# Moving the split of a group's row maxima from VectorE to GpSimd in a fused attention and expert block

## The chip, the cores and the metric

The kernel runs on one core of one Trainium2 chip. The metric is the device time of one launch in microseconds (us), the median of several runs. TensorE (PE) has its weight loads shown apart (PEld). VectorE is DVE, ScalarE is ACT, GpSimd is POOL, and SyncE (SP) only issues DMAs here. SPq and ACTq are the DMA issues from those two queues. Each engine works through its own list of instructions in order. Engines meet only at semaphores.

## What is computed

Four batches of 512 tokens of width 256 pass through a gated cross-attention and then a gated block of self-attention and experts. Both attentions have 16 heads of width 16:

```python
x = x + tanh(g_xattn) * xattn(layernorm(x), ctx, ctx, wq, bq, wk, bk, wv, bv)
x = x + tanh(g_ffn) * ffn(layernorm(x), ...)
# both attentions:
scores = einsum("bhld,bhsd->bhls", q, k) / 4
attn = softmax(scores, axis=-1)
out = einsum("bhls,bhsd->bhld", attn, v)
# ffn after its attention: rmsnorm(src + sa), shared swiglu experts,
# 8 routed experts in 2 groups, the best 2 of the best group, rmsnorm
```

## The kernel before

There are eight attention instances (four cross, then four self), and each has four **groups** of four heads: 32 groups, numbered 0 to 31 here. A group is worked through in 16 **steps** (4 tiles of keys by 4 heads). At each step PE makes one tile of transposed scores (the unit, L1754) and ACT takes its exponential (L949). After four of these PE multiplies them with the values (L1717, eight rows in the trace).

The exponential needs the row maxima of the scores beforehand. So PE also makes every score tile the other way round, 12 pairs ahead (L1689, two matmuls for a pair), and DVE takes the maximum of each row out of PSUM (L1205, writing `negm`). A pair goes through a ring of two bank pairs in PSUM. PE may fill one only when DVE has released the pair before last. Pairs are filled at the odd steps. A group's eighth and last pair is filled at step 7 of the group before it.

When all maxima of a group are there, they are parted into two bf16 numbers. `m2` (the trace calls it `m`) gets the rounded maximum (L1213, CAST) and then the rest of it (L1214, TENSOR_TENSOR), both 128 partitions by 16 elements. PE turns `m2` with one transpose (L1696, the **turn**) at step 9 (`AT_MAX`), ACT copies the result (L837), and at step 11 (`AT_ROWS`) ACT's queue issues two small DMAs (L846) that put the rows into the stack of queries. The first unit of the next group waits for these.

In between, at step 8 (`AT_HEADS`), PE turns the finished heads of the group before (L1703) through the same ring, and DVE divides them by their sums (L1226, L1227) and releases the bank. The next ring pair on PE waits for that.

What DVE has at a group's end, in its list: the maximum of the eighth pair (step 7), the two parts, the heads (step 8), the maximum of the next pair (step 9).

POOL does the parts of the projections (L684, L689, L694, 128 by 1024 elements each), the scale of each row of a norm (`row_scale`, a chain of small operations that ends in L677 or L679), the sum of heads (L704, L705) and, early on, a long row of memsets and iotas for the sorting at the end (`constants`). A table of hooks sets at which step of which group each piece is written on each engine. `link` on POOL and DVE lets an operation finish before the next one starts.

SP's list is in order too. While instance 0 runs it loads the stacks of groups 2 and 3, each when the rows of an earlier group have landed (`s_mrow`, L548 to L556). Only then does it store instance 1's parts to DRAM (L532, L538) and load them back as stacks.

Of the kernel before, what the change touches and what calls it, by code (L numbers as in the profile page):

```python
# [10 lines left out]
ALU = mybir.AluOpType  # L11
# [7 lines left out]
MPART = 2  # L19
# [3 lines left out]
LEAD = 12  # L23
FILL, FILL_STACK, FILL_ROWS = 24, 12, 10
PROB_SLOTS = 3
AT_COPY, AT_HEADS, AT_MAX, AT_ROWS = 4, 8, 9, 11
SCORE_BANKS = [0, 1, 7]
END_BANKS = [0, 1, 7, 6, 2, 3, 4, 5]

# [7 lines left out]
def flamingo_block(nc, x, ctx_in, g_xattn, g_ffn, wq, bq, wk, bk, wv, bv,  # L37
# [7 lines left out]
    NG = NH // HG  # L45
# [4 lines left out]
    EPG = NE // NGRP  # L50
# [13 lines left out]
    PAIRS = NH * TT // 2  # L64
    UNITS = NH * TT
    STEPS = UNITS // NG
# [5 lines left out]
    MROWS = MPART * HG * TT  # L72
# [5 lines left out]
    GROUPS = NI * NG  # L78
    N_PAIRS = NI * PAIRS
# [30 lines left out]
    for n in range(1, NI):  # L110
        m = n + 1
# [22 lines left out]
    for u_ in range(NI * UNITS):  # L134
        n_, g_, s_ = u_ // UNITS, u_ // STEPS % NG, u_ % STEPS
# [99 lines left out]
    with es:  # L235
        def sb(name, shape, dt):
            return es.enter_context(nc.sbuf_tensor(name, shape, dt))

        def sem(name):
            return es.enter_context(nc.semaphore(name))  # L240
# [58 lines left out]
        negm = sb("negm", [P, 2, HG, TT], F32)  # L299

        m2 = sb("m2", [P, 2, P], BF16)
# [91 lines left out]
        s_re = sem("ring_emptied")  # L393
        s_m2 = sem("maximum_parts")
# [32 lines left out]
        s_ini = sem("dve_setup_chain")  # L427
# [2 lines left out]
        block = es.enter_context(nc.Block())  # L430


        turned, taken = [], LEAD
        for gi_ in range(GROUPS):
            for s_ in range(STEPS):
                taken += s_ % 2 and (gi_ * STEPS + s_) // 2 + LEAD < N_PAIRS
                if s_ == AT_HEADS and gi_ > 0:
                    taken += 1
                    turned.append(taken)
# [31 lines left out]
        def group_inst(gi):  # L471
            return INST[gi // NG]
# [171 lines left out]
        def _(pool):  # L644
            k = [0]

            def link(ins):
                k[0] += 1
                ins.then_inc(s_pool, 1)
                pool.wait_ge(s_pool, k[0])  # L650
# [41 lines left out]
            def third_part(m, X):  # L692
                pool.wait_ge(s_p1[X], m + 1)
                link(pool.tensor_tensor(parts[X][:, 2], qk[X][:], parts[X][:, 1], ALU.subtract))  # L694
                pool.sem_inc(s_spl[X], 1)
# [3 lines left out]
            def add_heads(b, g):  # L699
# [6 lines left out]
                if g == NG - 1:  # L706
                    pool.sem_inc(s_x1, 1)

            def stats(m):
                kind, b = INST[m]  # L710
                row_scale(b, "x" if kind == "c" else "x1")
# [41 lines left out]
            for X in (1, 0):  # L753
                rest(1, X)
                third_part(1, X)
            pool.wait_ge(s_tg, 1)
            pool.memset(fg[:, :, NR:RW], 0.0).then_inc(s_cst, 1)
            constants()
            for n in range(NI):
                for g in range(NG):  # L760
                    gi = n * NG + g
                    for s in range(STEPS):
                        if s == AT_HEADS and gi > 0 and group_inst(gi - 1)[0] == "c":
                            add_heads(group_inst(gi - 1)[1], (gi - 1) % NG)
                        for what, m, i in HOOKS.get((n, g, s), []):
                            if what == "stats":
                                stats(m)
                            elif what == "sum":
                                rotated_sum(m, i)
                            elif what == "rest":  # L770
                                rest(m, i)
                            elif what == "part2":
                                third_part(m, i)
                            elif what == "fastats":
                                row_scale(m, "y")
# [253 lines left out]
        def _(dve):  # L1029
            k = [0]  # L1030

            def mark(ins):
                k[0] += 1
                ins.then_inc(s_dve, 1)

            def settle():
                dve.wait_ge(s_dve, k[0])

            def link(ins):
                mark(ins)  # L1040
                settle()

            def ready(s):
                settle()
                dve.sem_inc(s, 1)  # L1045

            V = nc.vector
# [152 lines left out]
            def row_max(q):  # L1200
                gi, p = divmod(q, PAIRS // NG)
                h, tt = divmod(p, TT)
                c, bank = ring.take()
                dve.wait_ge(s_rf, c + 1)
                V.tensor_reduce(negm[:, gi % 2, h::2, tt], ps[:, bank:bank + 2, :], AX.X, ALU.max,  # L1205
                                negate=True).then_inc(s_re, 1)
                if p + 1 == PAIRS // NG:
                    dve.wait_ge(s_re, c + 1)
                    if gi == 0:
                        dve.wait_ge(s_ini, 5 + EPG)  # L1210
                    m = negm[:, gi % 2].rearrange("p (a h) t -> p a (h t)", a=2)
                    o = m2[:, gi % 2, 0:MROWS].rearrange("p (a s r) -> p s a r", a=2, s=MPART)
                    link(V.tensor_copy(o[:, 0], m))  # L1213
                    mark(V.tensor_tensor(o[:, 1], m, o[:, 0], ALU.subtract))  # L1214
                    ready(s_m2)

            def heads_out(gi):
                kind, b = group_inst(gi)
# [35 lines left out]
            for n in range(NI):  # L1254
                for g in range(NG):
                    gi = n * NG + g
# [705 lines left out]
```

## Time and profile before

| | |
|---|---|
| median of 3 runs | 764.12 us (764.07 to 764.27) |
| the profiled execution, its own time | 764.05 us |
| its span, first to last instruction | 762.3 us |
| time outside the span | 1.75 us |
| PE busy, share of the span | 94% |
| DVE busy | 66% |
| ACT busy | 55% |
| POOL busy | 29% |
| mean granted clock of PE | 0.989 |

The attention with its 32 groups fills the span up to about 523 us; the experts follow. A row of the timeline gives the start in us from the span's start, the duration in us, engine, line, operation, output and input, shapes, how many instructions are merged in it, and in brackets how long the engine was idle before it and what ended that. A matmul row's duration is modelled. Weight loads (PEld) are apart from one another by about 0.23 us even when nothing is waited for, so such a row says that PE waits only where it stands clearly above that. A row of a grouped view gives busy us and mean ns of one instruction behind the first bar, and idle us before it behind the second.

### The profile page before, as it was taken

To read this page: it belongs to the slowest core of one execution; us is meant where nothing else is said; L and a number is where in the kernel's file an instruction comes from. 1 tells how busy PE (TensorE), PEld (TensorE's weight loads), DVE (VectorE), ACT (ScalarE), POOL (GpSimd) and SP (SyncE) were. 2 spreads that over 40 slices of the span, in tenths; PEclk is the share of its full clock that TensorE was granted. 3 is DMA by queue.
4 is the path that set the end of the run, shared out by engine and by line. 5 is a ranking of instruction groups with operands and counts; after the bars stand their busy time and mean duration, and the time that the engine had idled before them with its cause. 6 is when DMAs were issued, how large, how long until landed. Compare 5 with 4: busy or idle time off the path is not lost.

```text
span 762.3 us, 10523 instructions
## 1 busy us (share of the span) xinstructions
PE 718.1 (94%) x3470; PEld 319.1 (42%) x3512; DVE 505.9 (66%) x743; ACT 416.2 (55%) x800; POOL 221.7 (29%) x328
## 2 busy tenths in 40 slices
PE   8798999999999999999989999999999999999995
PEld 5432233243232233233323332424544856468884
DVE  5598758956968978977797789771476122533554
ACT  4356868777767876875775867676211122222111
POOL 7343133314305415303321510010104722400444
PEclk9999999999999999999999999999999999999998
DMA  8516514216214413322331332006002655000001
GB/s 262 186 43 213 162 51 166 85 39 208 80 43 157 146 46 121 118 82 83 108 92 43 107 112 75 10 3 209 12 1 112 215 176 166 0 1 0 36 35 42
DMA packets 61172, 73.33 MB, mean 96 GB/s; under 512 B 10944, under 2 KB 46016, under 8 KB 61120
## 3 DMA queue, kind: packets, MB, share of 16 engines
q1 hardware_dynamic: 56464, 63.81, 27.1%
q0 software_dynamic: 2816, 8.46, 3.0%
q10 hardware_dynamic: 1840, 0.40, 0.3%
q8 instruction: 29, 0.48, 0.3%
q14 instruction: 23, 0.19, 0.1%
HBM read 45.04 MB, written 27.33 MB: 95 GB/s over the span
## 4 chain that ended last, share of the span: by engine, by line
PE 65%; DVE 13%; ACT 8%; DMA 4%; issue 4%; SPq 2%; POOL 2%; ACTq 0%; POOLq 0%; DVEq 0%
PE ps L1558 30%; PE ps L1717 12%; PE ps L1754 11%; DVE negm L1205 7%; PE ps L1689 6%; ACT hS L949 5%; PE ps L1553 3%; POOL scrf L779 2%; DMA scrq<-mix 1%; DVE bst L1083 1%; PE ps L1703 1%; PE ps L1617 1%; DMA rows<-in_L_xattn_wq_dram 1%; DMA w<-scrq 1%; PE ps L1648 1%
## 5 line engine op out<-in xcount | busy, mean ns | idle before, releaser
L1205 DVE TENSOR_REDUCE negm<-ps 128x2 f32<-128x1024 f32 x256 | 302.7, 1221 | 67.0 <-PE ps L1689 58.5
L949 ACT ACTIVATE hS<-ps 128x512 f32<-128x512 f32 x512 | 280.4, 605 | 105.4 <-PE ps L1754 98.3
L1754 PE MATMUL ps<-w 98*128 98x512 bf16 (+1 forms) x470 | 160.7, 387 | 15.6 <-ACT hS L949 9.8
L1717 PE MATMUL ps<-hS,mix 128*17 128x512 f32 x1024 | 136.4, 605 | 0.2
L1689 PE MATMUL ps<-w 64*128 64x512 bf16 x512 | 100.3, 389 | 9.7 <-DVE negm L1205 4.9
L1754 PEld LDWEIGHTS ps<-w 98*128 98x128 bf16 (+1 forms) x512 | 43.5, 96 | 156.8 <-ACT hS L949 86.1
L1406 DVE SCALAR_TENSOR_TENSOR ctxs<-qk,ps 128x512 f32<-128x512 f32 x32 | 22.0, 687 | 72.4 <-ACT qk L985 71.6
L1689 PEld LDWEIGHTS ps<-w 64*128 64x128 bf16 x512 | 24.7, 93 | 95.4 <-issue 68.9
L985 ACT ACTIVATE qk<-ps 128x512 f32<-128x512 f32 x32 | 19.1, 597 | 76.3 <-PE ps L1558 76.3
L1558 PE MATMUL ps<-w,hS 128*128 x256 | 55.6, 379 | 0.0
L1558 PEld LDWEIGHTS ps<-w,hS 128*128 128x128 f32 x256 | 48.6, 190 | 7.0 <-issue 0.5
L666 POOL TENSOR_TENSOR mdif<-bst 128x4 f32<-128x4 f32 x12 | 2.5, 205 | 142.4 <-DVEq L1045 142.4
L689 POOL TENSOR_TENSOR qk<-qk,mix 128x1024 f32<-128x1024 f32 x14 | 29.8, 2131 | 47.8 <-ACT mix L869 47.4
L704 POOL TENSOR_SCALAR hS<-hS,tg 128x256 f32<-128x256 f32 x16 | 14.8, 928 | 92.2 <-DVEq L1231 92.2
L684 POOL TENSOR_TENSOR qk<-qk,hT 128x1024 f32<-128x1024 f32 x8 | 18.8, 2349 | 75.3 <-DVEq L1045 75.3
L694 POOL TENSOR_TENSOR mix<-qk,mix 128x1024 bf16<-128x1024 f32 x14 | 29.8, 2131 | 21.1 <-ACT mix L873 20.0
L1025 ACT ACTIVATE tmp<-mix 128x257 f32<-128x257 f32 x16 | 6.7, 418 | 49.9 <-DVE mix L1438 49.9
L1717 PEld LDWEIGHTS ps<-hS,mix 128*17 128x17 f32 x1024 | 17.0, 95 | 30.1 <-ACT hS L949 14.8
L1409 DVE SCALAR_TENSOR_TENSOR hS<-ctxs,ps 128x512 f32<-128x512 f32 x32 | 22.0, 687 | 10.3 <-PE ps L1558 10.0
L1558 PE MATMUL ps<-cT,fin 128*128 128x512 f32 x64 | 28.4, 594 | 0.3 <-ACT cT L978 0.3
L1558 PE MATMUL ps<-rope_sb,fin 128*128 128x512 f32 x64 | 28.4, 594 | 0.0
L779 POOL DMA_INDIRECT scrf<-rows,place x16 | 16.2, 1014 | 41.3 <-DVEq L1045 36.8
(220 smaller groups left out, 893.5 us busy)
## 6 DMA issues: line engine op xcount, KB each, us to landing
w<-scrk SPq DMA_DIRECT2D x192, 64.0 KB, 2.0
w<-scrq SPq DMA_DIRECT2D x64, 128.0 KB, 2.5
scrk<-mix SPq DMA_DIRECT2D x24, 256.0 KB, 2.5
scrq<-mix SPq DMA_DIRECT2D x16, 384.0 KB, 3.5
scrq<-mix SPq DMA_DIRECT2D x24, 256.0 KB, 2.5
w<-scrq SPq DMA_DIRECT2D x64, 64.0 KB, 2.5
w<-in_L_ffn_W_experts_dram SPq DMA_DIRECT2D x8, 512.0 KB, 8.2
mix<-scrf SPq DMA_DIRECT2D x4, 528.0 KB, 3.8
```

What stands on the lines that cost most here:

```text
L689: link(pool.tensor_tensor(qk[X][:], qk[X][:], parts[X][:, 0], ALU.subtract))
L694: link(pool.tensor_tensor(parts[X][:, 2], qk[X][:], parts[X][:, 1], ALU.subtract))
L779: pool.indirect_dma_start(dst[:], bass.IndirectOffsetOnAxis(ap=place[:, tile:tile + 1], axis=0), source, None).then_inc(done, 16)
L949: nc.scalar.activation(prob[:, kt % PROB_SLOTS, s % HG, :], slot_bank(("unit", u)), ACT.Exp, scale=SC).then_inc(s_exp, 1)
L1205: V.tensor_reduce(negm[:, gi % 2, h::2, tt], ps[:, bank:bank + 2, :], AX.X, ALU.max, negate=True).then_inc(s_re, 1)
L1406: V.scalar_tensor_tensor(out=uu[:, k % 2, :], in0=th[k % 4], scalar=1.0, in1=end_full(f"{name}{b}", 2 * p), op0=ALU.add, op1=ALU.mult).the ...
L1409: V.scalar_tensor_tensor(out=hS[:, b * TT:(b + 1) * TT, p, :], in0=uu[:, k % 2, :].rearrange("p (t j) -> p t j", t=TT), scalar=0.5, in1=en ...
L1553: last = TR(o[:, tt * P:(tt + 1) * P], t[:, tt, c * P:(c + 1) * P], identf[:])
L1558: last = MM(o, w, r, start=(j == 0), stop=(j == len(terms) - 1))
L1689: last = MM(ps[:, bank + kind, :], qs[at:at + MAIN, g, hh, tt * P:(tt + 1) * P], ks[at:at + MAIN, g, hh, :], start=True, stop=True)
L1717: last = MM(ps[32 * h:32 * h + VM, 6, :], vp[n % 2][:, kt, g * HG + h, :], prob[:, kk % PROB_SLOTS, h, :], start=(kt == 0), stop=(kt == TT ...
L1754: MM(o, ks[0:rows, g, h, kt * P:(kt + 1) * P], qs[0:rows, g, h, :], start=True, stop=True).then_inc(s_sT, 1)
```

## The change

The two operations leave `row_max` on DVE and become `max_parts` on POOL, with the same operands. They wait there for the release of the last pair of the group (`RING_AT` gives its number in the ring). They stand ahead of step 7's hooks of the group before (`AT_PARTS`); those of group 0 stand between POOL's parts of the keys and of the queries in the beginning.

```diff
-AT_COPY, AT_HEADS, AT_MAX, AT_ROWS = 4, 8, 9, 11
+AT_COPY, AT_PARTS, AT_HEADS, AT_MAX, AT_ROWS = 4, 7, 8, 9, 11
...
+        RING_AT = list(range(LEAD))
         turned, taken = [], LEAD
         for gi_ in range(GROUPS):
             for s_ in range(STEPS):
-                taken += s_ % 2 and (gi_ * STEPS + s_) // 2 + LEAD < N_PAIRS
+                if s_ % 2 and (gi_ * STEPS + s_) // 2 + LEAD < N_PAIRS:
+                    RING_AT.append(taken)
+                    taken += 1
...
+            def max_parts(gi):
+
+                pool.wait_ge(s_re, RING_AT[(gi + 1) * PAIRS // NG - 1] + 1)
+                if gi == 0:
+                    pool.wait_ge(s_ini, 5 + EPG)
+                m = negm[:, gi % 2].rearrange("p (a h) t -> p a (h t)", a=2)
+                o = m2[:, gi % 2, 0:MROWS].rearrange("p (a s r) -> p s a r", a=2, s=MPART)
+                link(pool.tensor_copy(o[:, 0], m))
+                link(pool.tensor_tensor(o[:, 1], m, o[:, 0], ALU.subtract))
+                pool.sem_inc(s_m2, 1)
...
             for X in (1, 0):
                 rest(1, X)
                 third_part(1, X)
+                if X:
+                    max_parts(0)
             pool.wait_ge(s_tg, 1)
             pool.memset(fg[:, :, NR:RW], 0.0).then_inc(s_cst, 1)
             constants()
...
                     for s in range(STEPS):
+                        if s == AT_PARTS and gi + 1 < GROUPS:
+                            max_parts(gi + 1)
                         if s == AT_HEADS and gi > 0 and group_inst(gi - 1)[0] == "c":
                             add_heads(group_inst(gi - 1)[1], (gi - 1) % NG)
...
                 V.tensor_reduce(negm[:, gi % 2, h::2, tt], ps[:, bank:bank + 2, :], AX.X, ALU.max,
                                 negate=True).then_inc(s_re, 1)
-                if p + 1 == PAIRS // NG:
-                    dve.wait_ge(s_re, c + 1)
-                    if gi == 0:
-                        dve.wait_ge(s_ini, 5 + EPG)
-                    m = negm[:, gi % 2].rearrange("p (a h) t -> p a (h t)", a=2)
-                    o = m2[:, gi % 2, 0:MROWS].rearrange("p (a s r) -> p s a r", a=2, s=MPART)
-                    link(V.tensor_copy(o[:, 0], m))
-                    mark(V.tensor_tensor(o[:, 1], m, o[:, 0], ALU.subtract))
-                    ready(s_m2)
```

Below, three places in the order of instructions. The semaphores in brackets are by their names in the program: `ring_emptied` is DVE's release of a pair, `pool_chain` and `dve_chain` are the `link` of the two engines, `x1_row_statistics` tells POOL that DVE has the statistics of a norm. The line numbers of the changed kernel are higher by 3 on POOL up to L711, by 14 after `max_parts`, and by 18 or 9 on DVE.

POOL's list at the end of the constants, in the beginning, before:

```order
L742 MEMSET tabs 128x1
L743 MEMSET tabs 128x2
L744 MEMSET tabs 128x1
L704 TENSOR_SCALAR hS<-hS,tg 128x4x64 [waits heads_ready]
L705 TENSOR_TENSOR rows<-rows,hS 128x4x64 [waits pool_chain]
```

and of the changed kernel:

```order
L756 MEMSET tabs 128x1
L757 MEMSET tabs 128x2
L758 MEMSET tabs 128x1
L719 CAST m<-negm 128x2x8 [waits ring_emptied]
L720 TENSOR_TENSOR m<-negm,m 128x2x8 [waits pool_chain]
L719 CAST m<-negm 128x2x8 [waits pool_chain,ring_emptied]
L720 TENSOR_TENSOR m<-negm,m 128x2x8 [waits pool_chain]
L707 TENSOR_SCALAR hS<-hS,tg 128x4x64 [waits pool_chain,heads_ready]
```

The parts of groups 1 and 2 now stand behind the last memset of the constants.

POOL's list around the `row_scale` of a self-attention norm (group 19's turn follows it), before:

```order
L672 TENSOR_SCALAR mdif<-mdif 128x4 [waits pool_chain]
L673 TENSOR_TENSOR nvar<-nvar,mdif 128x4 [waits pool_chain]
L677 TENSOR_TENSOR scale<-nvar,mhalf 128x4 [waits pool_chain]
L679 TENSOR_TENSOR shift<-mean,scale 128x4 [waits pool_chain]
L684 TENSOR_TENSOR qk<-qk,hT 128x1024 [waits pool_chain,rotation_ready0]
```

and of the changed kernel:

```order
L676 TENSOR_TENSOR nvar<-nvar,mdif 128x4 [waits pool_chain]
L680 TENSOR_TENSOR scale<-nvar,mhalf 128x4 [waits pool_chain]
L682 TENSOR_TENSOR shift<-mean,scale 128x4 [waits pool_chain]
L719 CAST m<-negm 128x2x8 [waits pool_chain,ring_emptied]
L720 TENSOR_TENSOR m<-negm,m 128x2x8 [waits pool_chain]
L719 CAST m<-negm 128x2x8 [waits pool_chain,ring_emptied]
L720 TENSOR_TENSOR m<-negm,m 128x2x8 [waits pool_chain]
L687 TENSOR_TENSOR qk<-qk,hT 128x1024 [waits pool_chain,rotation_ready0]
```

The parts of group 19 come after the whole chain of the norm's scale.

DVE's list at the end of a group, before:

```order
L1205 TENSOR_REDUCE negm<-ps 128x2 [waits ring_full]
L1213 CAST m<-negm 128x2x8 [waits ring_emptied]
L1214 TENSOR_TENSOR m<-negm,m 128x2x8 [waits dve_chain]
L1226 RECIPROCAL rec<-ps 128x16 [waits dve_chain,ring_full]
L1227 TENSOR_TENSOR hS<-ps,rec 128x4x64 [waits dve_chain]
L1205 TENSOR_REDUCE negm<-ps 128x2 [waits ring_full,ring_emptied]
```

and of the changed kernel:

```order
L1223 TENSOR_REDUCE negm<-ps 128x2 [waits ring_full]
L1235 RECIPROCAL rec<-ps 128x16 [waits ring_full]
L1236 TENSOR_TENSOR hS<-ps,rec 128x4x64 [waits dve_chain]
L1223 TENSOR_REDUCE negm<-ps 128x2 [waits ring_full,ring_emptied]
```

The reciprocal of the heads follows the last maximum directly. PE's list is the same in both.

## Rows read from the trace of the kernel before

**Rows 1.** The page: engines' busy time and share; the chain that ended last, by engine

```profile
PE 718.1 (94%) x3470; PEld 319.1 (42%) x3512; DVE 505.9 (66%) x743; ACT 416.2 (55%) x800; POOL 221.7 (29%) x328
...
PE 65%; DVE 13%; ACT 8%; DMA 4%; issue 4%; SPq 2%; POOL 2%; ACTq 0%; POOLq 0%; DVEq 0%
```

**Rows 2.** Groups of instructions on DVE: the two parts

```profile
L1213 DVE CAST m<-negm 128x16 bf16<-128x16 f32 x32 | 11.7, 366 | 1.1
...
L1214 DVE TENSOR_TENSOR m<-negm,m 128x16 bf16<-128x16 f32 x32 | 5.6, 175 | 1.1
```

**Rows 3.** Timeline at the turn of group 19, behind a norm's `row_scale`

```profile
323.88 1.22 DVE L1205 TENSOR_REDUCE negm<-ps 128x2 f32<-128x1024 f32 x1
...
325.13 0.17 DVE L1213 CAST m<-negm 128x16 bf16<-128x16 f32 x1
...
325.34 0.17 DVE L1214 TENSOR_TENSOR m<-negm,m 128x16 bf16<-128x16 f32 x1
...
325.63 0.10 PEld L1696 LDWEIGHTS ps<-identb,m 128*128 128x128 bf16 x1 [0.29 <-DVEq L1045]
...
325.76 0.20 POOL L679 TENSOR_TENSOR shift<-mean,scale 128x4 f32<-128x4 f32 x1
...
326.43 0.10 PEld L1689 LDWEIGHTS ps<-w 64*128 64x128 bf16 x2 [0.63 <-DVE hS L1227]
```

**Rows 4.** Groups of instructions on POOL and on DVE: prices of elementwise work

```profile
L694 POOL TENSOR_TENSOR mix<-qk,mix 128x1024 bf16<-128x1024 f32 x14 | 29.8, 2131 | 21.1 <-ACT mix L873 20.0 <-POOL mix L694 0.7 <-POOL rows L705 0.4
...
L705 POOL TENSOR_TENSOR rows<-rows,hS 128x256 f32<-128x256 f32 x16 | 11.6, 726 | 1.3
...
L666 POOL TENSOR_TENSOR mdif<-bst 128x4 f32<-128x4 f32 x12 | 2.5, 205 | 142.4 <-DVEq L1045 142.4
```

```profile
L1110 DVE TENSOR_TENSOR mix<-qk,mix 128x1024 bf16<-128x1024 f32 x2 | 2.5, 1226 | 0.3
```

**Rows 5.** Timeline at the turn of group 1: DVE, PEld and the last constant

```profile
55.17 0.17 DVE L1213 CAST m<-negm 128x16 bf16<-128x16 f32 x1
...
56.63 0.10 PEld L1696 LDWEIGHTS ps<-identb,m 128*128 128x128 bf16 x1 [0.34 <-issue]
```

```profile
59.51 0.10 POOL L744 MEMSET tabs<- 128x1 f32 x1
```

**Rows 6.** Chain that ended last at 58 us, and PEld at the stack's load

```profile
58.10 1.78 DMA w<-mTs
```

```profile
83.34 0.10 PEld L1689 LDWEIGHTS ps<-w 64*128 64x128 bf16 x2 [0.50 <-DMA w<-scrq]
```

**Rows 7.** Timeline: pauses of DVE and PE in the beginning

```profile
44.41 1.23 DVE L1205 TENSOR_REDUCE negm<-ps 128x2 f32<-128x1024 f32 x1 [0.56 <-DVE m L1214]
```

```profile
50.67 0.39 PE L1689 MATMUL ps<-w 64*128 64x512 bf16 x2 [1.05 <-DVE negm L1205]
```

```profile
75.28 0.59 PE L1754 MATMUL ps<-w 98*128 98x512 bf16 x2 [2.05 <-DMA w<-mTs]
```

**Rows 8.** Busy time by stretch: busy us (count) of each engine, PEclk, DMA share, GB/s

```profile
77.00:80.00 3.00, 3.00 (x14) 0.37 (x12) 1.59 (x2) 1.28 (x4) 0.29 (x2) 0.50 0.78 266
```

**Rows 9.** Timeline at the turn of group 17, with POOL at work

```profile
298.50 2.13 POOL L689 TENSOR_TENSOR qk<-qk,mix 128x1024 f32<-128x1024 f32 x1 [1.22 <-ACT mix L869]
299.07 1.59 DVE L1213 CAST m<-negm 128x16 bf16<-128x16 f32 x1
...
301.03 0.10 PEld L1696 LDWEIGHTS ps<-identb,m 128*128 128x128 bf16 x1 [0.23 <-DVEq L1045]
```

```profile
301.77 0.39 PE L1754 MATMUL ps<-w 128*128 128x512 bf16 x1 [0.50 <-ACT hS L949]
```

**Rows 10.** Timeline at the turn of group 29, with nothing else in the way

```profile
479.07 0.10 PEld L1696 LDWEIGHTS ps<-identb,m 128*128 128x128 bf16 x1 [0.23 <-DVEq L1045]
...
479.51 0.39 PE L1754 MATMUL ps<-w 128*128 128x512 bf16 x1 [0.21 <-ACT hS L949]
```

**Rows 11.** Timeline behind the turn of group 27: PE waits for DVE's ring

```profile
461.15 0.39 PE L1689 MATMUL ps<-w 64*128 64x512 bf16 x2 [0.72 <-DVE negm L1205]
```

## The prediction

> **What bounds the kernel now.** I read the page first: PE is busy 94% of the span and holds 65% of the chain that ended last, DVE 66% and 13% [rows 1]. PE runs its list in order, so what matters is whether a step of PE starts later or earlier, not how busy DVE is. DVE's share of the chain is the second thing to see: there are stretches in which PE waits for the ring. Then I read the groups of DVE for what leaves it: 32 casts of 0.366 us in the mean and 32 subtractions of 0.175 us, 17.3 us in all [rows 2]. Last I went through the timeline at all 32 turns, because the two operations have one consumer, the turn on PE. The question at each is what ends last there: the parts, PE's own work before the turn, or something else.
>
> Three kinds of turn are to be seen. In the plain kind [rows 10] the turn comes 0.23 us after the weight load before it, PE's usual spacing, so the parts are just in time or early, and 0.4 us later PE stands still for 0.21 us for an exponential that does not depend on the turn. In the second kind the parts are late: at group 19 the last maximum ends at 325.10, the parts at 325.51, and PE's load follows at 325.63, 0.53 us behind the maximum [rows 3]. In the third kind POOL is in the way: at group 17 a cast of normally 0.175 us takes 1.59 us and ends with POOL's operation, at 300.66 against 300.63 [rows 9].
>
> **What leaves DVE.** Two operations and their joints. At group 19 the cast starts at 325.13 and the heads' reciprocal could start there and not at 325.66, so 0.53 us for each group, and 1.4 us more where POOL blocks the cast. Little of it reaches the end: after nearly every turn DVE later stands idle for want of a pair, and the gain is gone by then. I found two places where DVE works without a pause from the turn to a wait of PE. One is behind group 27, where PE waits 0.72 us for the ring [rows 11]; the gain is the 0.53 us less what pair and DVE cannot move closer, -0.5 us. The other is group 0, where PE waits 1.05 us [rows 7], and it is part of the beginning, below.
>
> **What POOL's two operations cost.** POOL's nearest rows: a 128x4 tensor operation takes 0.205 us, a 128x256 one 0.726 us, 128x1024 to bf16 2.131 us [rows 4]. A line through the first two puts 16 elements at 0.205 + 12 x (0.726 - 0.205) / 252 = 0.23 us; I take 0.22 to 0.23, since 16 lies next to 4. The dear end for this shape is the row of 128x256, 0.73 us, the cheap end is DVE's own 0.175 us. With joints (about 0.1 us from a release to POOL's start, 0.08 between linked operations, 0.1 to PE; these are estimates from the gaps of 0.04 to 0.12 us between the rows of rows 3) the parts are ready 0.1 + 0.22 + 0.08 + 0.22 + 0.1 = 0.72 us behind the last maximum, against 0.53 now. So 0.2 us later where POOL is free, and never earlier. In the plain kind, six turns, the 0.21 us of idle time [rows 10] covers it: 0. In thirteen further turns PE comes later than the parts anyway: 0. Group 31 has no cover: +0.2.
>
> The Trainium skill speaks against this change: "GPSIMD Engine Reference", section "Engine selection", puts elementwise work on VectorE and calls GpSimd about twice as slow for two inputs. By it each operation would be twice 0.175, 0.35 us, and the parts 0.26 us later again than in my sum. The rows here say 2.131 against 1.226 us at 1024 elements, a ratio of 1.74, and 0.205 us at 4 elements.
>
> **The order on POOL** is the larger item. POOL runs in order, and the parts now stand behind whatever is written ahead of step 7.
>
> *Beginning.* Group 1's parts stand behind the constants. Their last memset ends at 59.61, while the last maximum is there when DVE's cast starts at 55.17; the turn loads at 56.63 [rows 5]. After: 59.61 + 0.03 + 0.22 + 0.08 + 0.22 + 0.1 = 60.26, which is 3.6 us later. PE's list stops there, and so does the other chain from the turn: ACT's copy, the DMA of the rows at 58.10, SP's stack loads and all of instance 1's stores and loads behind it, up to 83.34, where PE takes the stack with a wait of 0.50 (0.27 above the spacing) [rows 6]. Both move together, so 3.6 us reach the end. From this goes what group 0 gains: PE's pair at 50.67 waits for a DVE that saves 0.1 to 0.7 us before it (0.7 if the idle 0.56 us ahead of DVE's next maximum, at 44.41, goes with them [rows 7], hardly anything if that idle time has another cause), and POOL's work ahead of the constants hangs on that too. I take -0.4. To it comes the clock: after the pauses of 1.05 and 2.05 us [rows 7] PE's granted clock fell, to 0.50 in 77 to 80 us [rows 8], the 1.2 GHz level. A pause of 3 us will do the same; PE loses half of the some 3 us that it stays there, about 1.5 us, of which the wait for the loads hides most. I put +0.4 on it. Sum for the beginning: 3.6 - 0.4 + 0.4 = **+3.6 us** (2.9 to 4.7).
>
> *Four turns behind a `row_scale`* (groups 11, 15, 19, 23). At group 19 POOL's chain ends at 325.96 [rows 3], 0.86 us after the maximum. After: 325.96 + 0.1 + 0.22 + 0.08 + 0.22 + 0.1 = 326.68, 1.05 us behind today's 325.63. The next pair at 326.43 now waits for DVE's heads, but only 0.2 us of this can be given back, and ACT's copy and exponentials, which bound the steps that follow here, move by the whole 1.05. Three times 1.0, and 0.8 for group 23, where PE then waits a little for DVE anyway: **+3.8 us** (3.0 to 4.4).
>
> *Six turns with POOL at a projection's part* (groups 13, 17, 21, 25 like rows 9, and 14 and 18, where the cast took 0.39 us: the 11.7 us of rows 2 less the other thirty, halved). Today the cast sits behind POOL's operation, and after the change it still does. At group 17: 300.63 + 0.18 + 0.22 + 0.08 + 0.22 + 0.1 = 301.43, 0.4 us behind 301.03. There 0.50 us of PE's idle time follows [rows 9], so 0.1 us each; at 14 and 18 I reckon with less cover, 0.25 us each. **+0.9 us** (0.2 to 1.8).
>
> Sum: 3.6 + 3.8 + 0.9 + 0.2 (group 31) + 0.2 (plain turns that miss their cover) - 0.5 (group 27) = +8.2 us on the profiled 764.05: 772.2 us. That run lies within 0.1 us of the median, so the median should be **772.2**. With the terms at their ends: 769.5 to 776.5.
>
> **Rivals.** *The beginning is hidden.* PE has 2.05 us of waiting at 75.28 [rows 7], and if the rows' DMA and the stack loads had slack too, the 3.6 us would vanish there: 768.6. Against it: the loads hang on the same turn through SP, and the chain that ended last runs through them [rows 6].
> *POOL's small operations are dear.* By the ratio of 1.74 of rows 4, 0.305 us each, two operations 0.17 us more, on the 17 turns that could feel it (1 + 4 + 6, and six plain ones): +2.9, 775.1. By the skill's factor of two it would be 17 x 0.26 = 4.4, 776.6. By the 128x256 row, 17 x 1.0 = 17 us, 789; I leave that out of the range.
> *Faster.* DVE is what PE waits for in some stretches, and DVE gets 17 + 6 us of work and joints less. If the parts on POOL were nowhere later than today, PE's waits for the ring shrink; the few clear ones (1.05 and 0.72 us in rows 7 and 11, and some of 0.2 to 0.5 us) sum to some 5 us, so 759. It decides at one point: POOL must be free when the last maximum is there. At group 1 it is not, by 4.4 us [rows 5], and at the four `row_scale` turns by 0.86 us [rows 3].
> *No difference.* Delays that PE's and ACT's idle time eats all but, with DVE's gain against the rest: 764 to 765.5.
>
> **How the numbers follow.** My forecast 0.68; beginning hidden 0.10; dear operations 0.12; no difference 0.05; faster 0.05. A measurement here tells about 0.2% (1.5 us) from no change. Faster 0.05, same 0.05, slower 0.90. The range of 768.4 to 777.0 takes in the forecast's own range, the hidden beginning and the dear operations by both factors.
>
> **What would show it.** In the changed profile POOL's cast for group 1 starts at 59 to 60 us and PE's turn there loads at about 60, with an idle time of 3 us ahead of it on PE and a clock of 0.5 soon after; the stack's wait at 83.3 is at 86 to 87. The turns of groups 11, 15, 19, 23 are 1.5 to 1.6 us behind their last maximum, those of 13, 17, 21, 25 behind POOL's L692. Casts of m on POOL last 0.2 to 0.25 us. DVE is busy about 17 us less, POOL some 14 us more. The forecast is wrong if the casts on POOL take over 0.4 us, if the stack's wait does not move, or if the steps behind a late turn make up the time.

## The result

| | before | after |
|---|---|---|
| median | 764.19 us (764.07 to 764.62, 4 runs) | 773.44 us (772.93 to 774.04, 4 runs) |
| the profiled execution | 764.05 us | 773.47 us |
| its span | 762.3 us | 771.7 us |

The ratio is 1.0114, with an interval of 1.0096 to 1.0132 (ratios here are those on record and not the quotients of the two medians, which would be 1.0121 here): slower by 9.3 us, where 8.1 were forecast. In a later set of executions the changed kernel took 776.31 us against 764.50 (ratio 1.0150, 1.0126 to 1.0174), slower by 11.8 us. What is known of the difference between the two sets stands at the end.

The page of after, the rows that answer to [rows 1]:

```profile
PE 718.2 (93%) x3470; PEld 319.1 (41%) x3512; DVE 488.6 (63%) x679; ACT 416.9 (54%) x800; POOL 235.1 (30%) x392
...
PE 64%; DVE 11%; ACT 9%; POOL 7%; issue 4%; DMA 3%; SPq 1%; ACTq 1%; POOLq 0%; DVEq 0%
```

DVE lost the 17.3 us that were reckoned, POOL gained 13.4, and PE's busy time is the same to 0.1 us. So the 9.4 us stand in the profile as more idle time of PE, and POOL, at 30% busy, has risen from 2% to 7% of the chain. The instructions that touch `m` in after (minimum, median and maximum in ns), and below them what the engines waited for ahead of them (us, times):

```profile
L719 POOL CAST m<-negm x32: 196/196/197, 44.4 to 516.2; 128x16 bf16<-128x16 f32 x32
L720 POOL TENSOR_TENSOR m<-negm,m x32: 215/219/221, 44.6 to 516.5; 128x16 bf16<-128x16 f32 x32
...
  DVE negm L1223: 146.2, 21
  POOLq L721: 28.7, 34
```

The casts of 0.37 us in the mean [rows 2] are casts of 0.196 us now, all 32 of them. POOL had time for them at 21 groups, where it was idle until the maximum. At the other eleven it was not. Those are group 1, the four behind a `row_scale` and the six at a projection's part.

Timeline of after at the turn of group 1, which answers to [rows 5] and, in the last row, to the last of [rows 7]:

```profile
59.72 0.10 POOL L758 MEMSET tabs<- 128x1 f32 x1
59.76 0.20 POOL L719 CAST m<-negm 128x16 bf16<-128x16 f32 x1
60.04 0.22 POOL L720 TENSOR_TENSOR m<-negm,m 128x16 bf16<-128x16 f32 x1
60.36 0.10 PEld L1705 LDWEIGHTS ps<-identb,m 128*128 128x128 bf16 x1 [4.82 <-POOLq L721]
```

```profile
80.24 0.59 PE L1763 MATMUL ps<-w 98*128 98x512 bf16 x2 [2.10 <-DMA w<-mTs]
```

The cast stands right behind the last memset of the constants. PE's load had nothing before it for 4.82 us and came at 60.36, 3.73 us behind its place before. PE's wait for the rows' DMA is as long as before (2.10 against 2.05 us) and 4.96 us later: the chain through that DMA moved with the turn and hid nothing. The other wait, for the stack at 83.34 [rows 6], is gone:

```profile
88.11 0.10 PEld L1698 LDWEIGHTS ps<-w 64*128 64x128 bf16 x2 [0.32 <-issue]
```

PE comes there 4.77 us later than before, while SP issues the stack's load only 4.00 us later (83.04 against 79.04). So what was left of this wait, some 0.2 us, was hidden. The stretches of after there (columns as in [rows 8]) show the clock:

```profile
55.00:60.00 5.00, 0.39 (x2) 0.10 (x2) 2.96 (x9) 0.86 (x2) 4.67 (x58) 0.72 0.01 2
60.00:65.00 5.00, 4.63 (x19) 0.86 (x19) 1.37 (x2) 2.04 (x5) 0.22 (x1) 0.60 0.04 9
```

PE is busy 0.39 of 5 us and then works 5 us at a mean granted clock of 0.60, mostly the 1.2 GHz level. The mean over the whole span is 0.988 against 0.989 before. But from 40 to 100 us it is 0.91 against 0.94, and 1.00 in a second profile of before, so PE is slow for longer in the beginning. The slow time now lies behind the turn, where PE is late already.

Timeline of after at group 19, which answers to [rows 3], and at group 17, which answers to [rows 9]:

```profile
333.36 0.20 POOL L682 TENSOR_TENSOR shift<-mean,scale 128x4 f32<-128x4 f32 x1
333.73 0.20 POOL L719 CAST m<-negm 128x16 bf16<-128x16 f32 x1 [0.17 <-POOL shift L682]
334.01 0.22 POOL L720 TENSOR_TENSOR m<-negm,m 128x16 bf16<-128x16 f32 x1
334.33 0.10 PEld L1705 LDWEIGHTS ps<-identb,m 128*128 128x128 bf16 x1 [1.38 <-POOLq L721]
```

```profile
305.90 2.13 POOL L692 TENSOR_TENSOR qk<-qk,mix 128x1024 f32<-128x1024 f32 x1 [1.22 <-ACT mix L887]
...
308.20 0.20 POOL L719 CAST m<-negm 128x16 bf16<-128x16 f32 x1 [0.17 <-POOL qk L692]
308.48 0.22 POOL L720 TENSOR_TENSOR m<-negm,m 128x16 bf16<-128x16 f32 x1
308.80 0.10 PEld L1705 LDWEIGHTS ps<-identb,m 128*128 128x128 bf16 x1 [0.59 <-POOLq L721]
```

At group 19 the cast waits for the product that ends the norm's scale. PE waits 1.38 us where it waited 0.29. At group 17 PE waits 0.59 us, 0.36 above its spacing. The plain turn of group 29, which answers to [rows 10], shows the cover: the load stands at PE's usual spacing, and the pause behind it is 0.20 us, where it was 0.21:

```profile
488.20 0.10 PEld L1705 LDWEIGHTS ps<-identb,m 128*128 128x128 bf16 x1 [0.23 <-POOLq L721]
...
488.63 0.39 PE L1763 MATMUL ps<-w 128*128 128x512 bf16 x1 [0.20 <-ACT hS L967]
```

### Where the 9.4 us are

From here on each kernel is read in one way: the start of the turn's matmul is taken from the timeline for every group, and the same of before is subtracted. The table gives how this difference grows between turns, in us, for the profile of each kernel. Between the fourth turn and the last, two profiles of a kernel agree to 0.05 us but for the falls of the clock told below. "Four" are the steps into turns 11, 15, 19, 23 and "other" are all other steps from turn 4 to 26. "27" is the step from turn 26 to turn 28 (0.14 us later into turn 27, 0.73 sooner behind it), and "behind" is what lies behind the last turn.

| kernel | turn 0 | 0 to 4 | four | other | 27 | 29 to 31 | behind | sum |
|---|---|---|---|---|---|---|---|---|
| before, again | 0.52 | -0.71 | 0.01 | -0.02 | 0.00 | 0.00 | 2.74 | 2.5 |
| **after** | 0.86 | 4.08 | 4.11 | 0.66 | -0.59 | 0.14 | 0.12 | 9.4 |
| after, again | 3.44 | 3.92 | 4.12 | 1.52 | -0.59 | 0.14 | 0.04 | 12.6 |
| only group 1 | 1.95 | 5.02 | 0.00 | 0.03 | 0.00 | 0.00 | 0.31 | 7.3 |
| only the four | 0.64 | 0.01 | 4.52 | -0.08 | 0.00 | 0.00 | 0.17 | 5.3 |
| only the six | 2.45 | -1.00 | -0.03 | 0.69 | 0.00 | 0.00 | 0.06 | 2.2 |
| cast doubled | 1.89 | 4.83 | 4.98 | 4.01 | -0.24 | 0.31 | 0.12 | 15.9 |
| constants later | 0.67 | -1.30 | 4.11 | 1.56 | -0.60 | 0.14 | 0.20 | 4.8 |
| the same, all on DVE | 0.59 | 0.12 | 0.01 | 0.00 | 0.01 | 0.00 | 0.22 | 0.9 |
| only 0, 1, 2, 27 | -0.53 | 0.09 | 0.03 | -0.08 | -0.59 | 0.00 | 0.16 | -0.9 |
| mended order | 2.37 | -0.93 | 0.44 | 0.62 | -0.59 | 0.14 | 0.11 | 2.2 |
| mended, again | 2.09 | 1.50 | 0.44 | 0.64 | -0.60 | 0.13 | 0.01 | 4.2 |
| mended, seven on DVE | 1.39 | 0.57 | 0.86 | -0.04 | -0.59 | 0.00 | 0.33 | 2.5 |

### The profile page after: what moved, and what is told of

Read it like the earlier page. It is cut to its first block, busy times and chain, and to the rows that moved or that the text cites. A ratio compares the mean times of both kernels' runs of the same rounds, so it can differ in the third digit from the quotient of the medians.

```text
span 771.7 us, 10523 instructions
## 1 busy us (share of the span) xinstructions
PE 718.2 (93%) x3470; PEld 319.1 (41%) x3512; DVE 488.6 (63%) x679; ACT 416.9 (54%) x800; POOL 235.1 (30%) x392
## 4 chain that ended last, share of the span: by engine, by line
PE 64%; DVE 11%; ACT 9%; POOL 7%; issue 4%; DMA 3%; SPq 1%; ACTq 1%; POOLq 0%; DVEq 0%
PE ps L1567 30%; PE ps L1726 11%; PE ps L1763 10%; PE ps L1698 6%; ACT hS L967 6%; DVE negm L1223 5%; PE ps L1562 3%; POOL scrf L797 2%; POOL mix L697 1%; DVE bst L1101 1%; PE ps L1712 1%; DMA rows<-in_L_xattn_wq_dram 1%; PE ps L1626 1%; DMA w<-mTs 1%; ACT mix L891 1%
## 5 line engine op out<-in xcount | busy, mean ns | idle before, releaser
L719 POOL CAST m<-negm 128x16 bf16<-128x16 f32 x32 | 6.3, 196 | 147.9 <-DVE negm L1223 146.2
L1726 PEld LDWEIGHTS ps<-hS,mix 128*17 128x17 f32 x1024 | 17.0, 95 | 30.5 <-ACT hS L967 13.4
L818 POOL TENSOR_TENSOR rs<-ssq,mhalf 128x1 f32<-128x1 f32 x16 | 9.1, 567 | 65.0 <-ACT tmp L1043 65.0
```

What stands on the lines that cost most here:

```text
L1726: last = MM(ps[32 * h:32 * h + VM, 6, :], vp[n % 2][:, kt, g * HG + h, :], prob[:, kk % PROB_SLOTS, h, :], start=(kt == 0), stop=(kt == TT ...
```

## Experiments

My theory is that the price is POOL's order at a few places and PE's clock behind the first of them. One rival is that POOL's operations are dear at every turn. The other is that the beginning hides its delay.

### One part of the change at a time

The parts go to POOL for the groups of a set, and stay on DVE for the others. For the first kernel:

```diff
+PARTS_ON_POOL = {1}
...
-                        if s == AT_PARTS and gi + 1 < GROUPS:
+                        if s == AT_PARTS and gi + 1 in PARTS_ON_POOL:
...
                 V.tensor_reduce(negm[:, gi % 2, h::2, tt], ps[:, bank:bank + 2, :], AX.X, ALU.max,
                                 negate=True).then_inc(s_re, 1)
+                if p + 1 == PAIRS // NG and gi not in PARTS_ON_POOL:
```

with the eight lines of before under the last one.

> The parts of group 1 alone on GpSimd (behind the constants), all 31 others on VectorE as before. Theory: PE stops at group 1's turn until the constants are through, 3.6 us later than before, and everything behind it moves with it, the loads of instance 1 too; with the fallen clock 4.1 to 4.8 us slower than before, 768.3 to 769.0 us. Rival (the beginning is hidden behind the loads): 764.2 us.

Measured: 770.37 us, ratio 1.0084 (1.0063 to 1.0104), 1.4 us above the expected range. Its timeline at the turn, and its stretch behind it:

```profile
61.53 0.20 POOL L720 CAST m<-negm 128x16 bf16<-128x16 f32 x1
61.81 0.22 POOL L721 TENSOR_TENSOR m<-negm,m 128x16 bf16<-128x16 f32 x1
62.14 0.10 PEld L1715 LDWEIGHTS ps<-identb,m 128*128 128x128 bf16 x1 [5.31 <-POOLq L722]
```

```profile
60.00:65.00 5.00, 2.86 (x13) 0.49 (x13) 1.31 (x2) 1.35 (x3) 1.89 (x45) 0.50 0.02 4
```

One group of 32 makes more than half of the loss. Against the first profile of before, the turn comes 3.55 us later than it should behind turn 0, and from there to turn 4 another 1.47 us are lost, in stretches of which the first has a clock of 0.50. The 3.55 us match the 3.6 that were reckoned, but the split depends on the profile of before that is taken. The two differ in the stretch ahead of turn 1 (the first profile, then the second):

```profile
50.00:55.00 5.00, 3.92 (x18) 0.67 (x18) 5.00 (x5) 3.53 (x7) 1.96 (x1) 0.81 0.39 119
```

```profile
50.00:55.00 5.00, 3.55 (x21) 0.76 (x20) 5.00 (x5) 4.07 (x7) 1.86 (x2) 1.00 0.47 134
```

In the first profile the clock had fallen, and turn 1 came 0.96 us later behind turn 0 than in the second. By turn 2 this was made up: the two agree to 0.03 us there. Against the second profile the turn of group 1 is 4.51 us late here, and 1.21 us more are lost up to turn 4. What does not depend on the choice is the delay at turn 2, 5.22 us, for the constants and the clock together (4.05 and 5.15 us in the two profiles of after).

The second kernel has `PARTS_ON_POOL = {11, 15, 19, 23}`.

> The parts of groups 11, 15, 19 and 23 alone on GpSimd, behind a norm's row_scale. Theory: each of the four turns is 1.05 to 1.2 us later and nothing behind it makes that up: 4.4 us slower, 768.6 us. Rival (PE's and ACT's idle time takes half of it): 766.4 us.

Measured: 768.70 us, ratio 1.0065 (1.0052 to 1.0078). The steps are 1.17, 1.17, 1.10 and 1.09 us, and but for 0.04 and 0.03 us behind turns 19 and 23 nothing is given back. Its timeline at group 11:

```profile
206.94 0.20 POOL L683 TENSOR_TENSOR shift<-mean,scale 128x4 f32<-128x4 f32 x1
207.31 0.20 POOL L720 CAST m<-negm 128x16 bf16<-128x16 f32 x1 [0.18 <-POOL shift L683]
207.59 0.22 POOL L721 TENSOR_TENSOR m<-negm,m 128x16 bf16<-128x16 f32 x1
207.91 0.10 PEld L1715 LDWEIGHTS ps<-identb,m 128*128 128x128 bf16 x1 [1.46 <-POOLq L722]
```

The third has `PARTS_ON_POOL = {13, 14, 17, 18, 21, 25}`.

> The parts of groups 13, 14, 17, 18, 21 and 25 alone on GpSimd, behind a projection's part. As predicted: 0.9 us slower, 765.1 us. By the profile after, in which the delay of 0.36 us is given back behind the turn in four of the six: 0.3 us slower, 764.5 us. Rival (0.4 us at each of six): 766.6 us.

Measured: 765.54 us, ratio 1.0015 (1.0000 to 1.0030), which does not tell it from no change. The trace does:

```profile
242.46 0.20 POOL L720 CAST m<-negm 128x16 bf16<-128x16 f32 x1 [0.18 <-POOL qk L693]
...
243.06 0.10 PEld L1715 LDWEIGHTS ps<-identb,m 128*128 128x128 bf16 x1 [0.60 <-POOLq L722]
...
255.21 0.10 PEld L1715 LDWEIGHTS ps<-identb,m 128*128 128x128 bf16 x1 [0.59 <-POOLq L722]
```

These are turns 13 and 14, and all six of the kernel look like this: PE waits 0.59 or 0.60 us where it waited 0.23, so each of the six turns is 0.37 us late. The steps of the table show this only at 13, 17, 21 and 25. The start of each exponential behind the turns, against the second profile of before, tells what becomes of it. Behind turns 13, 17, 21 and 25 the whole 0.37 us are given back within the group (behind turn 13 two exponentials are 0.13 and 0.15 us late and the next 0.00). Turns 14 and 18 are then late anew, and behind them a part stays: 0.49 us by turn 15 and 0.20 us by turn 19, 0.69 us in all. In after the same two leave 0.12 and 0.20 us. So the 0.93 us that the table has for after at turns 15 and 19 are those turns' own 1.16 and 1.10 us less the 0.24 and 0.17 us that were given back since turns 14 and 18. Counted in this way the four turns cost 4.5 us in after as they do alone, and the six 0.3 us.

The three kernels add up: 5.02 + 4.52 + 0.69 = 10.2 us, against 4.08 + 4.11 + 0.66 = 8.9 us in after. Of the difference of 1.4 us, 0.9 are in the beginning, where after also has group 0 on POOL.

### The order on POOL mended

First in the beginning: the changed kernel, with the constants behind group 1's parts.

```diff
-            pool.memset(fg[:, :, NR:RW], 0.0).then_inc(s_cst, 1)
-            constants()
             for n in range(NI):
                 for g in range(NG):
                     gi = n * NG + g
                     for s in range(STEPS):
+                        if (gi, s) == (1, AT_HEADS):
+                            pool.memset(fg[:, :, NR:RW], 0.0).then_inc(s_cst, 1)
+                            constants()
```

> The changed kernel with the constants moved behind the parts of group 2 in GpSimd's list. Theory: group 1's turn follows its maximum at the usual 0.68 us; the 4.1 us of the beginning go, and group 0 keeps what VectorE gained there (PE's pause of 1.05 us and the clock's fall behind it are shorter): 773.4 - 4.1 - 1.5 = 767.8 us. Rival (the beginning cost nothing, the later turns all): 773.4 us.

Measured: 769.73 us, ratio 1.0087 (1.0074 to 1.0100). The beginning went from +4.08 to -1.30 us, 5.4 us less where 5.6 were expected. Still the median was 1.9 us above the expectation and the profiled execution, at 768.83 us, 1.0. The table shows 0.9 us of this: 1.56 instead of 0.66 us under "other". It lies between turns 23 and 24, where this kernel's instructions are those of after. The stretches there:

```profile
390.00:395.00 5.00, 2.87 (x18) 0.86 (x18) 4.79 (x9) 2.32 (x5) 3.97 (x13) 1.00 0.15 43
395.00:400.00 5.00, 4.54 (x18) 0.90 (x19) 3.39 (x7) 3.26 (x7) 0.20 (x1) 0.66 0.01 2
```

Behind the late turn of group 23 the clock fell to 0.66 and took 0.83 us. In the first profile of after it stayed at 1.00 at the same place. The other 0.9 us of the median stand in no profile.

The control has all parts on DVE and only the constants moved: the diff above with `PARTS_ON_POOL = set()`.

> The kernel before with all parts on VectorE, and only the constants of POOL written later, after group 1's step 8. It tells whether the -1.3 us that the beginning gained with the parts on POOL and the constants moved came from the parts or from the constants. My theory, from the parts (DVE's 0.56 us gap and PE's wait for the ring go): no difference here, 764.1 us, within 0.3. Rival, POOL's constants themselves slow the beginning (DVE's cast waited out POOL's operation at group 1 too): -0.5 to -1.3, so 762.8 to 763.6.

Measured: 765.52 us, ratio 1.0017 (1.0000 to 1.0033), and in the table little but the start. While DVE makes the parts, moving the constants alone gains nothing.

Then the four turns. The same kernel writes the parts of groups 11, 15, 19, 23 inside `row_scale`, ahead of the power:

```diff
+EARLY = {11, 15, 19, 23}
...
                 link(pool.tensor_tensor(nvar[:], nvar[:], mdif[:], ALU.add))
...
+                if between:
+                    max_parts(between)
                 link(pool.tensor_tensor(sc, nvar[:], mhalf[:], ALU.pow))
...
-                        if s == AT_PARTS and gi + 1 < GROUPS:
+                        if s == AT_PARTS and gi + 1 < GROUPS and gi + 1 not in EARLY:
...
                             if what == "stats":
-                                stats(m)
+                                stats(m, gi + 1 if gi + 1 in EARLY else None)
```

> All parts on GpSimd, but in a mended order: the constants behind group 1's parts, and at groups 11, 15, 19, 23 the parts written inside the norm's row_scale, ahead of its power (1.04 us) and its last product. My theory (these four turns are late by their place in POOL's list alone): the maximum is there at 332.70 while the chain's sum before the power ends at 332.17, so the parts wait for the maximum and not for POOL, each of the four turns is 0.14 us behind today's place on VectorE and not 1.05 to 1.18, and the +4.46 us fall to 0 to +0.6. The norm's scale comes 1.1 us later and nobody waits for it. With the beginning at -1.3, group 27 at -0.6, the six turns at +0.3 and group 31 at +0.1: 762.6 to 763.4 us. Rival (the four turns are late since GpSimd is slow at such work wherever it stands, or the norm's scale is awaited): 767 or more.

Measured: 766.06 us, ratio 1.0019 (1.0004 to 1.0033). Its timeline at group 11:

```profile
207.14 0.20 POOL L722 CAST m<-negm 128x16 bf16<-128x16 f32 x1 [0.60 <-DVE negm L1227]
207.41 0.22 POOL L723 TENSOR_TENSOR m<-negm,m 128x16 bf16<-128x16 f32 x1
207.73 0.10 PEld L1709 LDWEIGHTS ps<-identb,m 128*128 128x128 bf16 x1 [0.49 <-POOLq L724]
...
207.81 1.04 POOL L683 TENSOR_TENSOR scale<-nvar,mhalf 128x4 f32<-128x4 f32 x1 [0.18 <-POOL m L723]
```

The same two operations on the same engine, but POOL now waits 0.60 us for DVE, and not DVE's maximum for POOL. The four steps fell from 4.11 us to 0.44, and the scale that comes later is waited for by nobody. So the loss at these turns was the place in POOL's list, and the engine's own price is the 0.21 us by which turns 11 and 23 are still late. (Turns 15 and 19 are too; the table shows nothing there because about as much of the delay of turns 14 and 18 is given back ahead of them.) The time is 3 us above the expectation: 2.4 us of it are the late turn 0 of the profiled execution, ahead of everything that was edited against the kernel with the constants moved.

With groups 13, 14, 17, 18, 21, 25 and 31 put back on DVE (`gi + 1 not in EARLY | ON_DVE`, and DVE's eight lines for these seven):

> The same mended order, and the parts of groups 13, 14, 17, 18, 21, 25 and 31 left on VectorE. My theory: the six give back their +0.3 us and group 31 its +0.14, so 0.4 us less than the kernel with all parts on GpSimd: 762.2 to 763.0. It can beat the kernel before by 1 to 2 us, about what the landing of the first loads scatters. Rival (the moves only ever cost): 764 or more.

Measured: 765.89 us, ratio 1.0017 (1.0000 to 1.0033). The 0.62 and the 0.14 us are gone from the table, and 0.42 came back at the four, where the 0.2 us of a late turn stand alone now. The sum cannot be told from its neighbour. It is 3 us above its expectation, where the rival that every move costs has it.

Last, as the version that might beat both: parts on POOL for the groups 0, 1, 2 and 27 alone, with the constants moved.

> Parts on GpSimd for groups 0, 1, 2 and 27 alone, the other 28 on VectorE as before, and the constants written after group 1's step 8, behind the parts. My theory (the cost is POOL's order at a few places, the gain is VectorE's time at the few others): the beginning as with the constants moved, -1.3 us, the turn of group 27 -0.6 us, nothing anywhere else: 762.3 us, with 0.6 us of doubt for the landing of the first loads. Rival (each move to POOL costs, the gain is scatter of single profiles): 764 or more. By either the casts that stay on DVE last 0.37 us in the mean.

Measured: 764.63 us, ratio 1.0000 (0.9982 to 1.0018), where 762.3 us was expected and 764 or more was the rival's. Group 27 gave its 0.59 us in the trace. The beginning lost 0.09 us where a gain of 1.3 was expected, although turn 2 came 1.56 us sooner behind turn 0:

```profile
81.36 0.10 PEld L1709 LDWEIGHTS ps<-w 64*128 64x128 bf16 x2 [2.19 <-DMA w<-scrq]
```

```profile
80.00:85.00 5.00, 3.47 (x14) 0.52 (x15) 2.87 (x3) 1.55 (x4) 1.66 (x2) 0.69 0.54 145
```

PE reached the stack before its load and waited 2.19 us, and then ran at a clock of 0.69. No version beats the kernel before by an amount that can be measured.

### The price of POOL's operations

The changed kernel with the cast issued twice:

```diff
-                link(pool.tensor_copy(o[:, 0], m))
+                for _ in range(2):
+                    link(pool.tensor_copy(o[:, 0], m))
```

> The changed kernel with POOL's cast of the maxima issued twice, so the parts are ready 0.28 us later at every group (0.20 for the cast, 0.08 for the joint). My theory: the 0.28 us passes to the end in full at groups 1, 11, 15, 19, 23 and 31 (1.7 us), in part at 13, 14, 17, 18, 21, 25 (0 to 1.0) and at the six plain turns (0.07 each beyond their 0.21 us of idle time, 0.4 us): +2.1 to +3.1 us against the changed kernel, so 775.5 to 776.5. Rival, every turn feels POOL's price: 32 x 0.28 = +9 us, 782. Rival, the price is nothing and only the place counts: 773.4.

> The changed kernel unchanged, beside the others on the same chip, as the mark for the run with the doubled cast: 773.4 us, with the turns of groups 11, 15, 19, 23 in the same places to 0.02 us between themselves. What may differ is the start, where the landing of the first loads moved the turn of group 0 by 0.6 to 2.5 us between profiles.

Measured: 779.94 us, ratio 1.0198 (1.0173 to 1.0222), and 776.31 us, ratio 1.0150 (1.0126 to 1.0174), so the second cast costs 3.6 us. By the table it is more: 15.9 - 9.4 - 1.0 for the start = 5.5 us against the first profile of after. Most of it is of two kinds. The turns 11 to 25 other than 12, 16, 20, 22 and 24 pass 0.25 or 0.26 us each in full (0.10 at turn 11), since what is given back behind turns 13, 17, 21 and 25 is 0.37 to 0.39 us and no more. And the clock fell twice where it had not, behind turns 15 and 19, for 0.65 and 0.86 us:

```profile
274.00:278.00 4.00, 2.24 (x15) 0.52 (x15) 2.83 (x5) 1.90 (x4) 3.31 (x7) 0.93 0.24 77
278.00:282.00 4.00, 4.00 (x24) 0.60 (x16) 2.05 (x3) 3.56 (x8) 0.15 (x1) 0.64 0.01 2
```

The expectation of 2.1 to 3.1 us counted the six turns only in part and the falls of the clock not at all. The rival of every turn (+9 us) and that of no price are ruled out. The price that counts is 0.196 and 0.219 us, and it made little of the loss: 0.2 us at each turn without cover.

### How much of it is scatter

> The kernel before, profiled a second time. It tells whether the place of group 0's turn (44.51 us here, 43.98 to 47.95 us in the other kernels) is scatter of the start or comes from the edits. My theory, scatter: turn 0 somewhere in 44.0 to 48.0 us, all turns from the fourth on shifted by the same amount to 0.05 us, and the ratio to the runs beside it 1.000 to 0.002 either way. Rival, the edits move the start: turn 0 at 44.5 again.

> The mended order once more, beside the kernel before: 1.0019 was measured where the turns gave 0.2 us less than before once the start of 2.4 us is taken off. If the start is scatter, turn 0 lands elsewhere this time and the ratio comes out at 0.998 to 1.001. If the edit itself makes the start late (POOL's parts of group 0 ahead of its queries' parts), turn 0 is again at 46.5 us or later and the ratio at 1.002.

Measured: ratio 1.0001 (0.9983 to 1.0020) for the kernel before, 1.0024 (1.0007 to 1.0041) for the mended order. Turn 0 was at 45.03 and at 46.60 us, against 44.51 and 46.88. The kernel before also lost 2.74 us far behind the attention, between 604 and 614 us:

```profile
605.00:615.00 10.00, 8.48 (x36) 7.51 (x37) 0.00 (x0) 1.79 (x3) 4.82 (x6) 0.83 0.64 196
```

It has 9.36 us busy and a clock of 1.00 there in the first profile. So a single profile of one kernel scatters by 2.5 us in span (the kernel before) or 3.2 (after), all of it at the start, in the beginning and where the clock falls. The table is to be read with this: its columns from "four" to "29 to 31" repeat but for the falls of the clock, and those ahead of them and "behind" do not. For the mended order the text on record said that a second late turn 0 and a ratio of 1.002 speak for an edit that makes the start late, and that is what came. Against it stands that the kernel with the constants moved has the same lists up to there, and its turn 0 at 45.18 us. Whether the mended order is 0.2% slower for a reason or has had two late starts is open. The control with only the constants moved had 1.0017 as well, so their new place is one reason that is not ruled out.

## Why the prediction was right

The forecast of 772.2 us is 1.2 below the median of 773.44, inside its range, and its verdict of slower holds. Step by step, with the terms of the profiled run:

- **The delay in the beginning.** The constants end 14.35 us behind turn 0 in both profiles of after, and 15.00 to 15.03 us in the five that have group 0 on DVE and the constants in their old place. So group 0 gave 0.66 us and not 0.4, the upper end of what was allowed: the idle 0.56 us ahead of DVE's next maximum is 0.23 us in after. The turn of group 1 in after is 2.87 us late against the first profile of before and 3.83 against the second; 3.6 less 0.4 was the sum.
- **The clock in the beginning** is a mis-sized term: +0.4 was put on it. Between turns 1 and 4 the first profile of before gives 1.21 us for after and 1.47 for group 1 alone, the second 0.96 and 1.21. The step that was wrong is "of which the wait for the loads hides most". The wait for the rows moved with the turn and was as long as before, and the wait for the stack had 0.2 us to give. Sum for the beginning: 4.08 us (4.8 against the second profile of before) against 3.6, in the stated 2.9 to 4.7 or just above.
- **The four `row_scale` turns** had 3.8 us in the sum. They cost 4.5 us, alone and in after (4.11 in the table's way of counting), a little above the stated 4.4. The 1.05 us of group 19 were nearly right (1.09). What was given away was the reckoning of some give-back and of 0.8 for group 23, which cost 1.09. Next to nothing came back.
- **The six turns at a projection's part** had 0.9 us. In after they cost 0.3 us (0.66 in the table's way of counting), alone 0.69. The 0.4 us of lateness was right (0.37), and so was it that groups 14 and 18 have less cover than the other four. At 13, 17, 21 and 25 the cover was full, instead of 0.1 us left of each.
- **Group 27** had -0.5 and gave -0.59 us, **group 31** had +0.2 and cost 0.14, and the plain turns had +0.2 and cost nothing.
- **The start** is no term of the sum. It gave +0.86 us of the 9.4 of the profiled run. The other 8.5 us are near the forecast of 8.2 in part by luck: the beginning and the four turns came out 1.2 us dearer, the six and the plain turns 0.8 us cheaper.
- **The ends of the terms**, with the small terms as they stand, add up to 770.1 to 774.9 us and not to 769.5 to 776.5. The median of 773.44 lies in both, that of the later set, 776.31, only in the wider one.

Of the signs that were named, POOL's cast (59.76), PE's load (60.36) and the time that DVE lost came as said. The four turns loaded 1.61 to 1.69 us behind their maximum, where 1.5 to 1.6 was said. The idle time ahead of turn 1 was 4.82 us and not 3, and PE's load of the stack, named for 86 to 87 us, stood at 88.11 without a wait for it.

The 0.22 to 0.23 us put on POOL's operations came out at 0.196 and 0.219. The rule of the Trainium skill that stood against the change ("GPSIMD Engine Reference", section "Engine selection", about twice as slow for two inputs and roughly line-rate for one) gives the right verdict here for a reason that is not its own: at 16 elements the ratios are 0.196 to 0.175 us and 0.219 to 0.175 us [rows 2], 1.12 and 1.25. The prediction put the factor of two on the cast as well, which has one input, so its 776.6 us is more than the rule says. The rival of the hidden beginning is out by the one group that cost 5.0 us, the rival of dear operations by the rows of `m`, and the rival of a faster kernel fell at the point that was named for it: POOL was not free at group 1 and at the four. Where the order was mended so that it was, the gain that this rival promised did not come either: DVE's time is worth 0.59 us at group 27 and some 0.7 us at group 0.

## What to carry to other kernels

When a small operation moves to an idler engine, its price there hardly counts; what counts is what that engine has in its list ahead of it when the input is ready, place by place. Two operations of 0.42 us together cost some 4 us behind a row of memsets that nobody waited for, and 1.1 us behind a norm's scale, and nothing where the engine stood idle and the turn had cover. So the place in the list is to be chosen with the move. And a pause of PE is to be priced with the lower clock behind it.

## What was not expected of the hardware

- **The clock makes a pause cost more, at some times and not at others.** The five profiles in which all four turns were late have 20 such turns, with PE's matmuls idle for 1.1 to 1.4 us ahead of each. Behind four of them the clock fell to between 0.64 and 0.71 in a stretch of 4 or 5 us, and 0.65 to 0.86 us were lost. Behind the 36 turns of the same groups in the nine other profiles it never fell. The same kernel had the fall behind turn 23 in its second profile and not in its first. This and a start that is 2.6 us later are what sets the two profiled executions of the changed kernel, 773.47 and 776.63 us, apart. That they also separate the two sets (772.9 to 774.0 and 775.2 to 777.7 us, where the kernel before stayed at 764.19 and 764.50) is not shown. In the later set the mean granted clock was 0.984 to 0.987 in the changed kernel and 0.988 to 0.997 in the kernel before.
- **DVE's small cast waits out a large operation of POOL.** Before, four casts took 1.59 or 1.60 us and two 0.39 us, and all six ended within 0.04 us of POOL's operation [rows 9]. On POOL they take 0.196 us each time, and the parts come only 0.37 us later than they did, since DVE's cast had been waiting for the same end.
